# Routed expert tiles of a cross-attention and mixture-of-experts block: weight slices as the stationary operand of gate and up

## The reference

```python
logits = x_flat @ gate_w.T
scores = softmax(logits); w = scores * top2(scores)           # 8 experts, 2 kept
gu = einsum('nh,eih->nei', x_flat, experts_gate_up)           # h = 256, i = 2 * 352
g, u = gu[..., :352], gu[..., 352:]
h = silu(g) * u
expert_out = einsum('nei,ehi->neh', h, experts_down)          # back to 256
out = einsum('neh,ne->nh', expert_out, w)
out = out + sigmoid(x_flat @ shared_expert_gate_w.T) * shared_expert(x_flat)
```

## Time and profile before

| what | value |
|---|---|
| time, median of 3 runs | 919.99 us (912.99 to 921.75) |
| time of the profiled execution | 922.79 us |
| its span, first to last instruction | 921.0 us |
| mean granted TensorE clock | 0.975 |
| TensorE matmul busy | 814.9 us (88%), 8812 matmuls |
| TensorE weight load busy | 527.7 us (57%) |
| VectorE busy | 585.3 us (64%) |
| ScalarE busy | 407.9 us (44%) |
| POOL busy | 378.7 us (41%) |
| DMA | 102.59 MB, mean 111 GB/s |

### The profile page before, as it was taken

The page is one execution under the profiler, slowest core; times in us unless marked ns, Lnnn a source line. Parts: engine busy times, 40 slices in busy tenths (PEclk is TensorE's granted clock), DMA queues, the critical chain, the costliest instruction groups (busy, mean ns, idle before and its releaser), DMA issues.

```text
span 921.0 us, 23991 instructions
## 1 busy us (share of the span) xinstructions
PE 814.9 (88%) x8812; PEld 527.7 (57%) x8812; DVE 585.3 (64%) x1245; ACT 407.9 (44%) x663; POOL 378.7 (41%) x559
## 2 busy tenths in 40 slices
PE   4789999888889889979898878999999999998866
PEld 3445555544555555544355546777777777655434
DVE  5766678877888887765656684444444444367757
ACT  4235566554555565554645432443344433432221
POOL 7231455877656655653242230111111111356552
PEclk9889999999999999998999899999999999999999
DMA  5564555544445443444122031222222222233542
GB/s 166 163 191 144 155 142 166 142 146 128 138 113 142 110 137 111 117 130 123 38 72 83 35 104 53 81 78 80 81 82 81 82 82 83 71 121 111 175 119 80
DMA packets 78036, 102.59 MB, mean 111 GB/s; under 512 B 15202, under 2 KB 59362, under 8 KB 77924
## 3 DMA queue, kind: packets, MB, share of 16 engines
q1 hardware_dynamic: 60412, 66.63, 25.0%
q0 software_dynamic: 9552, 26.10, 8.6%
q10 hardware_dynamic: 7960, 8.33, 3.1%
HBM read 62.35 MB, written 38.14 MB: 109 GB/s over the span
## 4 chain that ended last, share of the span: by engine, by line
PE 57%; DVE 25%; issue 8%; ACT 4%; another core or an unknown queue 3%; DMA 2%; ACTq 1%; DVEq 0%; SPq 0%
PE ps_st L1780 14%; DVE mx L938 9%; PE ps_st L1403 8%; PE ps_m L1804 8%; PE ps_m L1185 5%; PE ps_st L1045 4%; PE ps_m L1119 3%; PE ps_o L1414 2%; PE ps_o L1095 2%; PE ps_o L1762 2%; PE ps_st L1063 2%; PE ps_m L1414 1%; PE ps_o L1790 1%; PE ps_m L1790 1%
## 5 line engine op out<-in xcount | busy, mean ns | idle before, releaser
L938 DVE TENSOR_REDUCE mx<-ps_st 128x4 f32<-128x1024 f32 x128 | 155.5, 1216 | 50.0 <-PE ps_st L1063 21.1
L760 ACT ACTIVATE p<-ps_st 128x1024 f32<-128x1024 f32 x128 | 131.0, 1023 | 107.0 <-PE ps_st L1079 90.1
L1780 PE MATMUL ps_st<-fwh,p 128*128 x568 | 138.7, 313 | 2.2 <-DVE p L1680 2.2
L1509 POOL DMA_DIRECT2D sorted_out<-p x71 | 38.4, 541 | 218.5 <-ACT p L1559 214.3
L1780 PE MATMUL ps_st<-fwl,p 128*128 x284 | 88.8, 312 | 0.0
L1335 POOL DMA_INDIRECT expert_rows<-hrow,slot x64 | 65.0, 1015 | 44.6 <-DVE slot L1326 27.9
L1045 PE MATMUL ps_st<-maskq,identb 64*64 64x512 bf16 x512 | 53.6, 409 | 31.2 <-DVE mx L938 27.8
L1780 PEld LDWEIGHTS ps_st<-fwh,p 128*128 128x128 f16 x568 | 55.6, 98 | 29.0 <-issue 2.9
L1403 PE MATMUL ps_st<-q,arena 128*128 128x512 f16 x264 | 59.8, 379 | 9.1 <-issue 7.4
L1517 POOL DMA_INDIRECT p<-sorted_out,xn x52 | 53.0, 1019 | 32.6 <-DVE xr L1660 15.7
L1403 PE MATMUL ps_st<-qk,arena 128*128 128x512 f16 x264 | 60.6, 384 | 5.8 <-issue 3.0
(11 more groups left out here) (243 smaller groups left out, 2036.4 us busy)
## 6 DMA issues: line engine op xcount, KB each, us to landing
arena<-ffn_dram SPq DMA_DIRECT2D x20, 544.0 KB
p<-expert_rows SPq DMA_DIRECT2D x71, 128.0 KB, 2.1
sorted_out<-p POOLq DMA_DIRECT2D x71, 128.0 KB, 2.0
qk_scratch<-arena SPq DMA_DIRECT2D x32, 256.0 KB, 2.6
qk<-qk_scratch SPq DMA_DIRECT2D x44, 128.0 KB, 3.0
xr<-x_dram SPq DMA_DIRECT2D x8, 512.0 KB, 4.5
arena<-ctx_dram SPq DMA_DIRECT2D x16, 256.0 KB
hT_dram<-hT ACTq DMA_DIRECT2D x16, 256.0 KB
```

Source lines behind the costliest of these rows:

```text
L760: eng.activation(expo[n % 4][:, :, :], ps_st[pair["T", n]][:, :].rearrange("p (h q) -> p h q", h=4), ACT.Exp, scale=SCALE).then_inc(s_e, 1)
L938: eng.tensor_reduce(mx[b % 2][:, qt, :].rearrange("p (h g j) -> p h g j", h=2, g=HG)[:, :, hg, :], ps_st[pair["S", 8 * b + n]][:, :].rearr ...
L1780: last = mm(o[:, 0:INTER], xgT[k % 2][:, xl, dc, :], (fwh, fwl)[wl][:, bass.ds(e, 1), w0 + dc * INTER:w0 + (dc + 1) * INTER], start=dc == ...
```

## The change

In gate and up of the routed tiles the operands swap roles. The weights are now the stationary operand, in slices of 128 features by 128 inner units, and `xgT` moves with its 128 columns (rows of the tile). The product comes out with the inner units on partitions, as down needs it. So there are 3 chunks of inner units by 2 chunks of features by 3 terms, for gate and for up.

The three transposes of `hf`, the semaphore `r_ht`, the two memsets and the semaphore `r_pad` go. ScalarE makes `hh` and VectorE `hl` straight from `hf` in on-chip memory. Silu and the product run over 384 columns instead of 352. A slice of the third chunk reads 32 columns beyond the 352 of its weights; what they give lies on partitions 96 to 127, and down leaves these out (`real`), with a stationary operand of 96 partitions in its third chunk.

```diff
@@ scalar, routed tile k
-                    eng.activation(gs[k % 2][:, 0:INTER], ps_g[k % 2][:, 0:INTER], ACT.Silu).then_inc(r_si, 1)
+                    eng.activation(gs[k % 2][:, 0:NC * P], ps_g[k % 2][:, 0:NC * P], ACT.Silu).then_inc(r_si, 1)
                 if 0 <= k - 1 < NTILE:
-                    eng.wait_ge(r_ht, k)
+                    eng.wait_ge(r_hf, k)
...
-                    eng.activation(hh[(k - 1) % 2][:, :, 0:P],
-                                   ps_d[1 + (k - 1) % 2][:, 0:3 * P].rearrange("p (c t) -> p c t", c=3),
+                    eng.activation(hh[(k - 1) % 2][:, :, 0:P], hf[(k - 1) % 2][:, 0:NC * P].rearrange("p (c t) -> p c t", c=NC),
                                    ACT.Copy).then_inc(r_hh, 1)
@@ vector
-            for i in range(2):
-                eng.memset(hf[i][:, INTER:3 * P], 0.0).then_inc(r_pad, 1)
-            eng.wait_ge(r_pad, 2)
...
                     if k >= 2:
-                        eng.wait_ge(r_ht, k - 1)
-                    eng.tensor_tensor(hf[k % 2][:, 0:INTER], ps_u[k % 2][:, 0:INTER], gs[k % 2][:, 0:INTER],
+                        eng.wait_ge(r_hl, k - 1)
+                    eng.tensor_tensor(hf[k % 2][:, 0:NC * P], ps_u[k % 2][:, 0:NC * P], gs[k % 2][:, 0:NC * P],
                                       ALU.mult).then_inc(r_hf, 1)
...
-                    eng.tensor_tensor(hl[b % 2][:, :, 0:P], ps_d[1 + b % 2][:, 0:3 * P].rearrange("p (c t) -> p c t", c=3),
+                    eng.tensor_tensor(hl[b % 2][:, :, 0:P], hf[b % 2][:, 0:NC * P].rearrange("p (c t) -> p c t", c=NC),
                                       hh[b % 2][:, :, 0:P], ALU.subtract).then_inc(r_hl, 1)
@@ tensor, gate and up
-                        for dc in range(DC):
-                            for wl, xl in TERMS:
-                                last = mm(o[:, 0:INTER], xgT[k % 2][:, xl, dc, :],
-                                          (fwh, fwl)[wl][:, bass.ds(e, 1), w0 + dc * INTER:w0 + (dc + 1) * INTER],
-                                          start=dc == 0 and (wl, xl) == (0, 0), stop=dc == DC - 1 and xl == 1)
+                        for c in range(NC):
+                            for dc in range(DC):
+                                at = w0 + dc * INTER + c * P
+                                for wl, xl in TERMS:
+                                    last = mm(o[:, c * P:(c + 1) * P], (fwh, fwl)[wl][:, bass.ds(e, 1), at:at + P],
+                                              xgT[k % 2][:, xl, dc, :], start=dc == 0 and (wl, xl) == (0, 0),
+                                              stop=dc == DC - 1 and xl == 1)
                         last.then_inc(s_out, 1)
-                if 0 <= k - 1 < NTILE:
-                    b = k - 1
-                    eng.wait_ge(r_hf, b + 1)
-                    if b >= 2:
-                        eng.wait_ge(r_hl, b - 1)
-                    for c in range(3):
-                        last = eng.transpose(ps_d[1 + b % 2][:, c * P:(c + 1) * P], hf[b % 2][:, c * P:(c + 1) * P],
-                                             ident[:, :])
-                    last.then_inc(r_ht, 1)
@@ tensor, down
-                    for c in range(3):
-                        at = DOWN0 + c * D
+                    for c in range(NC):
+                        at, real = DOWN0 + c * D, slice(0, IC[c])
                         for wl, xl in TERMS:
-                            last = mm(ps_d[3][:, 0:D], (hh, hl)[xl][b % 2][:, c, 0:P],
-                                      (fwh, fwl)[wl][:, bass.ds(e, 1), at:at + D],
+                            last = mm(ps_d[3][:, 0:D], (hh, hl)[xl][b % 2][real, c, 0:P],
+                                      (fwh, fwl)[wl][real, bass.ds(e, 1), at:at + D],
```

More of the change, by code:

```diff
@@ L1465, in ffn @@
         r_t = sem("r_t"); r_tx = sem("r_tx"); r_g = sem("r_g"); r_u = sem("r_u"); r_si = sem("r_si"); r_hf = sem("r_hf")
-        r_ht = sem("r_ht"); r_hh = sem("r_hh"); r_hl = sem("r_hl"); r_y = sem("r_y"); r_ys = sem("r_ys")
-        r_pad = sem("r_pad")
+        r_hh = sem("r_hh"); r_hl = sem("r_hl"); r_y = sem("r_y"); r_ys = sem("r_ys")
         r_st = [sem(f"r_st{i}") for i in range(3)]
@@ L1737, in down @@
                     eng.wait_ge(r_ys, NTILE)
-                    eng.wait_ge(r_hl, NTILE)
                 for j in range(BT):
@@ L1800, in _ @@
                     e = experts.pop(b)
-                    for c in range(3):
-                        at = DOWN0 + c * D
+                    for c in range(NC):
+                        at, real = DOWN0 + c * D, slice(0, IC[c])
                         for wl, xl in TERMS:
-                            last = mm(ps_d[3][:, 0:D], (hh, hl)[xl][b % 2][:, c, 0:P],
-                                      (fwh, fwl)[wl][:, bass.ds(e, 1), at:at + D],
-                                      start=c == 0 and (wl, xl) == (0, 0), stop=c == 2 and xl == 1)
+                            last = mm(ps_d[3][:, 0:D], (hh, hl)[xl][b % 2][real, c, 0:P],
+                                      (fwh, fwl)[wl][real, bass.ds(e, 1), at:at + D],
+                                      start=c == 0 and (wl, xl) == (0, 0), stop=c == NC - 1 and xl == 1)
                     last.then_inc(r_y, 1)
```

## The result

The changed kernel takes 1021.26 us (median of 4 runs, 1016.16 to 1024.12), the kernel before 918.93 beside it (4 runs, 912.99 to 921.75): a ratio of 1.112, 95% interval 1.105 to 1.119. It is slower by 102 us. 1015 had been forecast.

What follows compares the result with a forecast made beforehand. The array bound the kernel at 3.32 us per tile; the sequencer would bind the changed one at 4.70. Terms +95.6, +1.2 and -0.4 gave +96.4, taken as +95: 1015 us from 919.99, range 975 to 1040.

Steps and rivals of the forecast that it cites:

- What bounded before: Routed tiles before the change: TensorE's array at 3.32 us per tile, its sequencer under that at 2.9 us.
- The price of an address instruction: TensorE's sequencer: each address for a new weight slice takes 0.12 us, from starts 0.13 and 0.125 apart.
- Their number: Gate and up: 24 address instructions per tile in place of 8, each serving high and low; 16 more, 1.92 us.
- Rival 4: Gate and up: no load's address is used twice, so 36 per tile, 1.44 us more; 1115 us, chance 0.05.
- The array's part: TensorE's array: 36 matmuls of gate and up take 2.01 us in place of 1.79; the tile needs 3.21, 0.11 less.
- Rival 3: Gate and up: loads of 98 ns don't hide behind short matmuls, the tile takes 4.73 us; 1019 us, chance 0.07.
- The sequencer's tile: TensorE's sequencer per tile: 2.9 + 1.92 for 16 addresses - 0.12 for a wait = 4.70 us, becoming the bound.
- The sum: First gate to last: two tiles of 4.2 and 68 of 4.70 us, 328.0 in place of 232.4, +95.6 us.
- the second in line: VectorE's copy of `xgT` for the next tile would set 3.40 us per tile if the sequencer didn't bind.
- rival 1: Addresses don't bind, being folded or hidden; the copy of `xgT` sets 3.40 us per tile; 926 us, chance 0.09.
- a lower clock in ten tiles: Clock falling to 1.2 GHz as the array idles: 36 matmuls take 3.8 us, +10 us for ten such tiles.
- Rival 2: The array sets the time at 3.21 us per tile if the sequencer stays below that; -8, 912 us, chance 0.06.

Runs made afterwards that it cites:

- the third-chunk run: Changed kernel with only the third chunk of inner units of gate and up read from expert 0 at a fixed address; 922.54 us against 887.02 for the kernel before.
- fixed addresses: Gate and up of every tile read expert 0's weights: changed kernel so altered 882.68 us against 887.02 for the kernel before; kernel before so altered 888.46 against 888.26.
- the paired run: Changed kernel reading the expert's number every second tile only, the odd tile reusing the even one's weights and addresses; 923.62 us against 888.26 for the kernel before.

## Why the prediction was right

**What bounded before** was the array, with the sequencer near behind: confirmed from both sides, by 8 addresses less (no change) and 7 more (+33).

**The price of an address instruction**, 0.12 by starts and not 0.03 to 0.05 by durations, was the step on which everything hung. Measured between the change and the third-chunk run: 0.121.

**Their number**, 24 per tile with high and low served by one: 852 of each kind. Rival 4 (36) is out by this count.

**The array's part**, 2.01 for 36 matmuls and 3.21 for the tile: 2.01 and 3.22 where the addresses were fixed. Rival 3 is out: 36 in a row keep 0.056 here.

**The sequencer's tile**, 4.70 forecast, 4.79 measured. The term that was short is the price of one instruction. The two rows gave 0.13 and 0.125, and the prediction took 0.12. With 0.125 for the 16 new addresses and the wait, its own sum is 2.9 + 2.0 - 0.125 = 4.78. In the changed kernel's trace the address instructions of gate and up start 0.127 apart in the mean of all tiles: seven in eight come 0.112 to 0.125 after the one before, the others later, up to 0.295. The 3.0 to 3.2 that the chain shows for the 36 matmuls can't be set against the prediction's 2.8: it also holds the wait ahead of the row transposes, and 24 x 0.12 is 2.88. The load of the expert's number gave nothing back. Its median of 302 ns is about the 320 that the 2.9 held:

```profile
L1764 PEldq TENSOR_LOAD <-qk x71: 295/302/492, 554.8 to 889.5; - x71
```

**The sum.** From the first gate to the last 328.0 were forecast; it is 890.41 - 555.86 = 334.55, +102.1 on the 232.4 of before. Of the 6.5 us beyond the forecast, 6.3 are the 0.09 of 68 tiles. The two first tiles took 4.34 and 4.31 where 4.2 each were written, with 2.8 for 24 x 0.12; with 2.88 it is 4.32. The ends were sized about right, and small. That the +102.1 is the measured 102 is in part chance, since the profiled execution's span grew by 93.4 only. The profiled execution before (922.79) was slower than all four timed ones of that kernel, the one after (1016.16) was the fastest of its four. Its stretches outside the routed part were 9 us shorter than before, 6 of it behind the routed part, where the granted clock was higher; that the clock is the reason is not shown (the clock is the column ahead of the last two; the first row is the kernel before, the second the changed one):

```profile
795.00:921.00 126.00, 103.78 (x613) 60.31 (x611) 79.59 (x155) 32.60 (x56) 66.70 (x67) 0.96 0.39 116
```
```profile
888.00:1014.00 126.00, 108.03 (x682) 65.10 (x680) 82.17 (x160) 34.77 (x62) 68.21 (x68) 0.98 0.39 118
```

**What was wrong** is the second in line, 3.40 per tile from the copy of `xgT` (rival 1's time). With fixed addresses it measured 3.22 or less. Two terms were too long: copy to gate at most 0.48, not 0.60, once no address instruction stands between, and `hf` to copy 0.47, not 0.52. It changed nothing in the forecast, since the sequencer was slower still. Where addresses cost nothing it gave a loss of 0.08 per tile for what was a gain of 0.10. The range had +10 us for a lower clock in ten tiles, now that the array idles. No run shows that term: from 570 to 880, with such idle time in every tile, the granted clock was 1.00.

**Rival 2**, 8 us less from the array alone, has its mechanism shown: with fixed addresses it is 4 us less than before (3 to 8 by the interval), at 3.22 per tile. The condition it set, a sequencer below 3.21, is what the real kernel can't meet. 30 addresses at 0.12 are 3.6 us, before a wait or the expert's number is counted. Keeping addresses in registers over tiles of one expert may do it: the odd tiles of the paired run, which had no address to make for gate and up, took 3.22 (554.18 to 557.40). It was not tried with the tiles' true experts, and the program would have to branch for it.

## What to carry to other kernels

Price a change that cuts matmuls into smaller ones through a register on the sequencer, by counting different addresses, not matmuls: 7 more of them per tile cost 33 us here with the matmuls unchanged. Take the price from the distance between starts, in a stretch where the queue is empty; the durations in the record, 46 and 32 ns, are a third of the 0.121 us measured here. Don't round it down: 0.005 for each of 16 new instructions per tile was most of the miss here. When the idle time of an engine is put down to "issue" and its matmuls come in evenly spaced groups, count the register and wait instructions per tile against the tile's time; here removing a bounds check was worth 0.27 us per tile, and the work saved on the array nothing.

## What the runs showed of the hardware

Matmuls and loads cost the sequencer next to nothing: the old layout with 7 more addresses (28 pairs of load and matmul and 21 addresses per tile) takes 266.1 / 70 = 3.80 per tile, the changed kernel without the third chunk's (49 pairs, 22 addresses, one wait less) 268.3 / 70 = 3.83. The reading of the expert's number has a median of 494 ns in the kernel before and 302 in the changed one. It isn't that the sequencer runs ahead of a full array in the first: the runs with fixed addresses in either kernel, where it does too, have 302 and 304. Why it is longer in that one profile, no run tells. Nor do they tell why one address in eight starts later than 0.125 after the one before, or why taking 8 away saves 0.121 each where the mean distance of starts is 0.127.

24 address instructions of 46 and 32 ns, 0.94 us by the record, took 3 of 4.79 us per tile, in a stage where the record has TensorE busy for 92% and the array had 3.22 us of work per tile, 67%.
